# Two layers of adaptive scaling, experts and attention: border loads, table and final sums moved

## What is computed

```python
x = x + experts0(scaled_linear(x, cond))     # 8 experts, the best 2 of each token, plus shared ones
y = up(relu(down(x))) + x                    # adapter; its two weights are formed per sequence from cond
h = layernorm(y); z = y + attention(h) @ w_o + b_o
h = layernorm(z)
topv, topi = top_k(h @ gate_w + gate_b, 2); gw = softmax(topv)
x = x + z + sum over the two chosen e of gw * (relu(h @ W1[e] + b1[e]) @ W2[e] + b2[e])
```

## Time and profile before

| | |
|---|---|
| median of 3 runs | 739.51 us (737.39 to 741.89) |
| the profiled execution | 738.1 us, its span 736.3 us |
| busy share of the span | TensorE 80%, VectorE 67%, POOL 61%, ACT 50% |
| mean granted TensorE clock | 0.903 |
| moved by DMA | 115.24 MB, 157 GB/s over the span |

### The profile page before, as it was taken

One profiled execution on the slowest core, in us unless ns is written; L12 is line 12 of the kernel. 1 busy time (PEld: TensorE's weight loads), 2 busy tenths in 40 slices (PEclk: granted clock), 3 DMA queues, 4 the chain that ended last, 5 costly groups with the idle time before them and its releaser, 6 DMA issues. The chain is left out here.

```text
span 736.3 us, 17755 instructions
## 1 busy us (share of the span) xinstructions
PE 588.9 (80%) x5538; PEld 473.9 (64%) x5538; DVE 490.2 (67%) x1502; ACT 370.1 (50%) x798; POOL 448.7 (61%) x588
## 2 busy tenths in 40 slices
PE   4999935999992787737999999999920999999940
PEld 2566625989892555415766766676620999999940
DVE  3566434767671689755878878877652678878735
ACT  3444303655561344335777777777520556556520
POOL 2677741766677658274455887797763256666640
PEclk9999976999996599967999999999955899999985
DMA  7911146767773267715553444444117988888429
GB/s 223 244 57 52 55 94 163 213 198 207 201 212 103 71 187 220 222 68 104 102 119 85 132 108 132 105 125 123 44 40 162 314 258 246 260 242 248 138 66 314
DMA packets 97978, 115.24 MB, mean 157 GB/s; under 512 B 16144, under 2 KB 77616, under 8 KB 97776
## 3 DMA queue, kind: packets, MB, share of 16 engines
q1 hardware_dynamic: 82368, 92.36, 46.8%
q0 software_dynamic: 9088, 18.76, 7.8%
q10 hardware_dynamic: 6448, 3.20, 1.8%
HBM read 80.75 MB, written 33.53 MB: 155 GB/s over the span
## 5 line engine op out<-in xcount | busy, mean ns | idle before, releaser
L341 POOL DMA_INDIRECT dispatch_rows<-row,index x128 | 126.0, 984 | 56.9 <-issue 33.7
L825 POOL DMA_INDIRECT expert_rows<-fo,to x78 | 84.0, 1076 | 68.2 <-DVE fo L1883 54.8
L1570 DVE TENSOR_REDUCE mneg<-ps 128x4 f32<-128x512 f32 x128 | 86.6, 679 | 43.4 <-PE ps L1711 42.6
L825 POOL DMA_INDIRECT expert_rows<-eo,to x78 | 74.7, 958 | 52.6 <-ACT eo L918 30.2
L1661 ACT ACTIVATE prob<-ps 128x512 f32<-128x512 f32 x128 | 75.4, 589 | 54.2 <-PE ps L1723 53.5
L798 DVE CAST xh<-psT 128x256 fp32r<-128x256 f32 x78 | 33.1, 424 | 73.8 <-PE psT L766 73.6
L1872 PE MATMUL psO<-wb,fh 128*128 128x128 f32 x624 | 75.9, 275 | 0.0
L1711 PE MATMUL ps<-km,qp 96*128 96x512 f32 x128 | 63.2, 500 | 14.0 <-POOL km L1508 12.7
L1654 ACT ACTIVATE km<-kp,const 96x512 fp32r<-96x512 f32 x96 | 67.7, 712 | 11.0 <-PEq L1045 5.5
L816 PE MATMUL psA<-xh,wh 128*128 128x256 f32 (+1 forms) x234 | 73.1, 312 | 0.0
L1872 PEld LDWEIGHTS psO<-wb,fh 128*128 128x128 f32 x624 | 73.1, 192 | 0.0
(11 more groups left out here) (193 smaller groups left out, 1505.2 us busy)
## 6 DMA issues: line engine op xcount, KB each, us to landing
wb<-in_W1b SPq DMA_DIRECT2D x39, 578.0 KB
w<-in_W SPq DMA_DIRECT2D x39, 304.0 KB
qk_parts<-qk SPq DMA_DIRECT2D x8, 1024.0 KB, 5.0
qp<-qk_parts SPq DMA_DIRECT2D x48, 128.0 KB, 2.8
kp<-qk_parts SPq DMA_DIRECT2D x48, 128.0 KB, 3.4
qm<-qk_parts SPq DMA_DIRECT2D x192, 32.0 KB
xs<-dispatch_rows SPq DMA_DIRECT2D x39, 130.0 KB
xt<-dispatch_rows SPq DMA_DIRECT2D x39, 130.0 KB
```

The costliest lines, as they stand in the source:

```text
L341: pool.indirect_dma_start(out=m.xbuf, out_offset=bass.IndirectOffsetOnAxis(ap=r.index[b][:, c:c + 1], axis=0), in_=r.row[b][:, c // TOPK, ...
L825: pool.indirect_dma_start(out=m.ybuf, out_offset=bass.IndirectOffsetOnAxis(ap=to[b][:, a:a + 1], axis=0), in_=out[b][:, a, :], in_offset=N ...
L1570: nc.vector.tensor_reduce(mneg[s % 2][:, g, :], ps1[:, g % 2, :].rearrange("p (j k) -> p j k", j=4), AX_X, ALU.max, negate=True).then_inc( ...
```

## The change

It does five things.

1. **Table.** `table_vector` is cut into parts. In `layer0` the counts stand between the third gate of group 6 and the first of group 7, the experts behind that, the rows before the last gate, and the rest behind it. A new part (`table_sends`) works out how many sends of each result buffer belong to real tiles of experts 0 to 6 and of all experts. SP issues all 8 fills; ACT issues none.
2. **Border loads.** At the end of `layer0` and of `attention` SP loads the weights of tiles 0 and 1 as soon as the table is there, then waits for fills and scatters, and loads the rows of tiles 0 and 1 (`lead_loads`). The expert stages skip these. Their buffers, and those that pass from `experts0` to `pre_attention`, lie where both stages can use them (`shared_memory`, a buffer shared with attention's `prob`).
3. **Adapters.** In `experts0`, behind its tiles, SP loads the operands of groups 0 and 1, waits for the sends of the real tiles (`sends_done`), and loads these groups' rows. VectorE forms the two groups' weights and adds their rows. POOL and VectorE no longer do so in `pre_attention`.
4. **Halves.** In layer 1 a row's target is `SEQS * p + s`, plus 4096 for the expert with the higher number. So one half of `m.ybuf` is complete when the tiles of experts 0 to 6 have been sent.
5. **End.** `finish` is gone. In `experts1`, SP waits for each half's sends and loads it (4 transfers of 512 KB, pieces of 4 KB) into `m.V` and `m.X3`. VectorE adds both in place, 16 operations of 512 columns; ACT stores 8 groups of 256 KB. Some semaphores of the start are merged.

```diff
 def choose_hot(r, dve, n):
+    if r.halves:
+        nc.vector.tensor_tensor(r.later[b][:], r.choice[b][:, :, 0], r.choice[b][:, :, 1], ALU.is_gt)
...
 def index_place(r, dve, n, rank):
-    nc.vector.tensor_copy(r.row[side][:, :, :, SLOT_ID:SLOT_ID + 1].bitcast(U32),
-                          m.ids[:, n * GT:(n + 1) * GT, :].unsqueeze(3))
+    if r.halves:
+        rows = m.const[:, C_ROW:C_ROW + SEQS * TOPK].rearrange("p (s k) -> p s k", k=TOPK)
+        for k, half in ((0, float(TOK)), (1, -float(TOK))):
+            nc.vector.scalar_tensor_tensor(out=r.row[side][:, :, k, SLOT_ID].bitcast(U32), in0=r.later[b][:], scalar=half,
+                                           in1=rows[:, n * GT:(n + 1) * GT, k], op0=ALU.mult, op1=ALU.add)
...
-    table_fill(w, sp, range(E // 2))
-    sp.wait_ge(w.tails, 16 * (E + 1))
+    table_fill(w, sp, range(E))
...
+def table_sends(w, dve):
+    c(v.memset(w.real[:], 0.0))
+    for a in range(2):
+        ins = v.tensor_tensor(w.real[:, a, 0:ETILES], tl, bc(w.incl[:, E - 2 + a:E - 1 + a], P, ETILES), ALU.is_lt)
+    c(ins)
+    c(v.tensor_reduce(w.sends[:], w.real[:].rearrange("p a (i q) -> p a q i", q=OB), AX_X, ALU.add))
+    c(v.tensor_scalar(m.table[:, DONE:DONE + 2 * OB], w.sends[:].rearrange("p a q -> p (a q)"), 32.0, None, ALU.mult))
...
 # layer0, vector
+                    if n == GROUPS - 1:
+                        table_rows(tiles, dve)
                     gate(n, 2)
+                    if n == GROUPS - 1:
+                        table_sends(tiles, dve)
+                        table_end(tiles, dve)
                     if n + 3 < GROUPS:
                         scale(n + 3)
+                    if n == GROUPS - 2:
+                        table_counts(tiles, dve)
                     if n + 1 < GROUPS:
                         gate(n + 1, 0)
+                    if n == GROUPS - 2:
+                        table_experts(tiles, dve)
...
                 add(GROUPS - 1)
-                table_vector(tiles, dve)
...
+def lead_loads(m, sp, tiles, scattered, weights, w, xs):
+    sp.wait_ge(tiles.tabled, 1)
+    rows = []
+    for b in range(LEAD):
+        e = sp.value_load(m.table[0:1, b:b + 1], min_val=0, max_val=E - 1)
+        sp.dma_start(w[b], weights[bass.ds(e, 1)].rearrange("e p h -> (e p) h")).then_inc(m.ld[b], 16)
+        rows.append(sp.value_load(m.table[0:1, b + ETILES:b + ETILES + 1], min_val=0,
+                                  max_val=E * REGION + (E - 1) * SLOTS))
+    sp.wait_ge(tiles.tails, 16 * (E + 1))
+    for sem, total in scattered:
+        sp.wait_ge(sem, total)
+    for b in range(LEAD):
+        sp.dma_start(xs[b], m.xbuf[bass.ds(rows[b], SLOTS), :].rearrange("(a p) c -> p a c", p=P)).then_inc(m.ld[b], 16)
+
+def sends_done(m, sp, sent, layer, a):
+    for b in range(OB):
+        at = DONE + OB * a + b
+        sends = sp.value_load(m.table[0:1, at:at + 1], min_val=32 * (8 if a else 4), max_val=32 * 10)
+        sp.wait_ge(sent[b], sends + 32 * uses(b, OB) if layer else sends)
...
 # experts0, sync, behind the tiles
+                for b in range(2):
+                    sp.dma_start(gbu[b][:], m.gb_dram[b * GT:(b + 1) * GT, 2 * DOWN:].unsqueeze(0).to_broadcast(
+                        [DOWN, GT, 2 * P])).then_inc(m.gbu_in[b], 16)
+                sends_done(m, sp, st, 0, 1)
+                for b in range(2):
+                    sp.dma_start(rows[b][:], m.ybuf[b * GW * TOPK:(b + 1) * GW * TOPK, :].rearrange(
+                        "(t p k) c -> p t k c", p=P, k=TOPK)).then_inc(m.rows_in[b], 16)
...
 # experts0, vector, behind the tiles (four memsets of parts of wu and eight operations for both groups)
+                for b in range(2):
+                    dve.wait_ge(m.rows_in[b], 16)
+                    nc.vector.tensor_tensor(part[b][:], rows[b][:, :, 0, :], m.X[:, b * GT:(b + 1) * GT, :], ALU.add
+                                            ).then_inc(blend1, 1)
+                for b in range(2):
+                    dve.wait_ge(blend1, b + 1)
+                    nc.vector.tensor_tensor(m.x1[b], rows[b][:, :, 1, :], part[b][:], ALU.add).then_inc(blended, 1)
...
 # attention, sync, behind table_sync
+                sp.wait_ge(mixed, SEQS)
+                lead_loads(m, sp, tiles, [(sem, post.router.sends * GROUPS // 2) for sem in post.router.scattered],
+                           d["W1b"], m.late_w, m.late_xs)
...
 # experts1, sync, behind the tiles
+                for a, to in enumerate((m.V, m.X3)):
+                    sends_done(m, sp, st, 1, a)
+                    mine = m.ybuf[a * TOK:(a + 1) * TOK, :].rearrange("(p s) c -> p s c", s=SEQS)
+                    for h in range(HALVES):
+                        part = slice(h * HS1, (h + 1) * HS1)
+                        sp.dma_start(to[:, part, :], mine[:, part, :]).then_inc(upper[h] if a else lower, 16)
...
 # experts1, vector, behind the tiles
+                def blend(n, a):
+                    h, mine, rows, sem = n * GT // HS1, slice(n * GT, (n + 1) * GT), (m.V, m.X3)[a], m.blends[a]
+                    dve.wait_ge(upper[h] if a else lower, (0 if a and h else came_before) + (16 if a else 16 * HALVES))
+                    if a:
+                        dve.wait_ge(m.blends[0], GROUPS + n + 1)
+                    nc.vector.tensor_tensor(m.X[:, mine, :], rows[:, mine, :], m.X[:, mine, :], ALU.add).then_inc(sem, 1)
+                blend(0, 0)
+                for n in range(GROUPS):
+                    if n + 1 < GROUPS:
+                        blend(n + 1, 0)
+                    blend(n, 1)
...
 # experts1, scalar, behind the tiles
+                for n in range(GROUPS):
+                    act.wait_ge(m.blends[1], GROUPS + n + 1)
+                    act.dma_start(out_rows[n * GT:(n + 1) * GT].rearrange("s p c -> p s c"), m.X[:, n * GT:(n + 1) * GT, :]
+                                  ).then_inc(m.stored, 16)
```

More of the change, by code:

```diff
@@ L495, in _ @@
                 table_sync(tiles, sp)
+                lead_loads(m, sp, tiles,
+                           [(r.scattered[b], r.sends * len(range(b, GROUPS, ROW_BUFFERS))) for b in range(ROW_BUFFERS)],
+                           d["W123"], [w[:] for w in m.lead_w], [x[:] for x in m.lead_xs])
             @block.gpsimd
@@ L843, in experts0 @@
         psO = m.ps("psO0", [P, 2, 512], ctx)
-        m.ld = ld = [m.sem(f"e_ld{b}") for b in range(EB)]
+        ld = m.ld
         m.st = st = [m.sem(f"e_st{b}") for b in range(OB)]
@@ L1007, with adapter_sems @@
 PRE_LINKS = 3
+def adapter_sems(m):
+    m.rows_in = m.sems(*(f"rows_in{b}" for b in range(1 + HALVES)))
+    m.gbu_in = m.sems("p_gbu0", "p_gbu1")
+    m.mods = m.sems("p_mod1", "p_modded")
+    m.blends = m.sems("p_blend1", "p_blended")
 def pre_attention(m, d):
```

216 lines of the change are left out of this document (120 added, 96 removed).

## The result

The changed kernel takes 714.04 us (median of 4 runs, 712.37 to 715.25), the kernel before took 740.7 beside it: a ratio of 0.9637, 95% interval 0.9583 to 0.9691. Predicted were 708.3 and a range of 702 to 717. The gain is 26.7 us by the medians where 31.2 were worked out.

The account below looks back on a forecast made before the run. TensorE sets the pace inside stages, something else at the borders and end. Savings of 8.9 + 5.9 + 3.5 + 12.9 = 31.2 us from the profiled 738.1 give 706.9; the median's 1.4 more makes 708.3, range 702 to 717.

Parts of the forecast that it names:

- the four borders: The three borders between stages and the end, where TensorE has holes: 8.9 + 5.9 + 3.5 + 12.9 us saved.
- rival (a): SP's single queue bounds borders 1 and 3, fills landing 3 us later than taken in both: 714; chance 0.14.
- the four good ends: The most favourable savings at the three borders and the end: 10, 7.3, 4.5 and 14 us.
- Border 1: Dispatch to first expert stage: earlier table and weights leave only row loads behind the scatters; 8.9 us saved, 6 to 10.
- Border 2: First expert stage to adapters: early row loads, then VectorE's four additions, open the stage; 5.9 us saved, 2.2 to 7.3.
- The version kept in the range: Border 2: six padding sends each slowed 0.41 us beside VectorE's work, POOL ending 2.5 us later, leaving 4.8 of 5.9.
- Border 3: Attention to second expert stage: SP's eight fills land last, then only row loads and copies; 3.5 us saved, 2.5 to 4.5.
- The end: After the last tile: lower halves load early, then 16 additions at 0.70 us; 12.9 us saved, 9 to 14.
- (b): Early loads and padding sends delay each other; border 2 gives 2.2, the end 10: + 6.6, 715; chance 0.10.
- (c): Early waits complete only with the last tile's sends; border 2 gives 1, the end about 8: + 10, 718; chance 0.04.
- In between: Stretches between borders: two more small VectorE operations per group in attention, priced 0, at most 2.4 us; other parts 0.
- Rival (d): Layer 1 rows 16 KB apart make sends land later and VectorE wait; losing the gain takes 31 us; chance 0.03.

Follow-up runs that it names:

- the last kernel: Changed kernel plus fills on both queues, lower loads singly, POOL behind normalising, early clears, and unread TensorE products at layer ends and before tile 0: 710.24 us.

## Why the prediction was right, and where it was not

The mechanism of the four borders held; the stretches between them did not keep their length. Part of the nearness is luck. From trace to trace the gain is 23.1 against 31.2, a miss of 8.1, while the medians miss by 5.7: the prediction put the median 1.4 above the profiled execution, and for the changed kernel it lies 1.0 below. That 714 is also what rival (a) gave is chance as well, since the time went elsewhere. And the range's lower end is 1.7 us below what the four good ends give (703.7), so it was wider there than its own reason.

**Border 1 (8.9 predicted, 8.29 found, 8.95 when undone).** Right step by step, within 1.2 us. On its own axis the rows' loads left 4.1 us behind the last scatter (2.9 predicted), and from there to the first product took 4.3 us (4.9 predicted). The fills took 10.2 us instead of 8.2 and still ended before the scatters. Rival (a) is out here.

**Border 2 (5.9 predicted, 4.62 found, 5.2 when undone).** The side of VectorE was even quicker than worked out: on the axis of before its additions end at 232.5 (233.8 predicted). The step that failed is the one I had set aside for the range: that the padding's sends take their 0.96 beside VectorE's work. They took 1.60 and 2.71; 2.4 us more in sum, and POOL, not VectorE, opened the stage. The runs show it: 0.96 in all sends with VectorE's work taken away, 2.2 us gained at the border with the sends taken away, and VectorE's chain as long with them as without (8.19 and 8.26). The version kept in the range, six times the 0.41 of the earlier trace rows, gave 4.8, near the 4.62, but for another course: one of the six lost 1.75, another 0.64, the rest 0.1 or less. The Trainium skill, page "SBUF — State Buffer", section "SBUF: two separate sides", says that VectorE's two-port operations keep GpSimd from writing descriptors. The trace does not bear that out as the reason: everything that VectorE runs beside the two stretched sends is `tensor_tensor`, to which the same section gives no two-port mode, and while its clears and first products run (216.23 to 220.34) the sends took 0.95 to 1.04. Nor does an unbroken row of `tensor_tensor` always stretch a send: two of 0.96 stand beside the sixteen additions at the end. That VectorE's work did it is shown; by which operations and when is open.

**Border 3 (3.5 predicted, 2.25 found).** The fills' issue was right (8.48 us, 8.6 predicted). The mis-sized term is the way from the last scatter to the first transpose: 8.6 us where 7.4 were worked out. The last scatter was down 6.0 us after its issue, not 2.8, and the last fill 6.2 after its own, not 5.0; so SP waited for the scatter in the end, not for the fills. The rows' loads left 1.9 us later than worked out, but in two other traces they left as predicted (3.9 and 4.3) and the transpose came no sooner. The prediction took a free way for all these transfers; the weights' 1.2 MB go out right behind the fills and share the engines. Rival (a) named the place, but on the quick chip not the cause: with two queues the border was the same (10.58 against 10.63 to 10.86). On the slow kind it was 2.0 shorter, and there rival (a) was true. That on the quick chip it is the bytes fits all traces, but was not tested.

**The end (12.9 predicted, 14.16 found, 14.2 when undone).** The additions were sized at 0.70 and took 0.61 each, 1.4 us in sixteen; the halves never kept VectorE waiting. Rivals (b), for the end, and (c) are out.

**In between (0 predicted, 7.1 lost).** This is the larger miss. The sum took it that a stage in which TensorE sets the pace, or which the change does not touch, keeps its length. 2.9 us of it are the adapters: VectorE's busy time in the eight groups is 51.82 us where it was 49.12,

```profile
234.00:292.00 58.00, 45.55 (x243) 30.37 (x242) 51.82 (x136) 23.44 (x41) 34.72 (x38) 0.90 0.54 165
```

```profile
246.50:301.60 55.10, 45.61 (x243) 30.25 (x242) 49.12 (x135) 23.44 (x41) 36.72 (x38) 0.89 0.63 178
```

with the same operations: they meet POOL's at a worse moment. The normalising takes 2.2 to 3.2 us in four of the eight groups, in two before. It was seen in every kernel that has the change (56.6 to 59.3 us for eight groups, 55.1 in the one trace of before), also in the one with the adapters' part undone (58.7), so it is not that part's own price; a new phase between the engines is the reading that is left. That holding POOL back does not cure it was shown; what sets the phase was not.

1.6 us are the second expert stage: undoing the halves and the end gave 2.0 back, spreading the loads nothing. Kernels that leave this stage alone took 147.0 to 147.5 us on the first chip, where undoing gave 145.05, and 146.0 and 147.9 on the second, where the loads were spread. Rival (d), rows 16 KB apart, is not seen at its price of 31 us: in both traces of the quicker kind a pair of tiles takes 6.9 us from the third pair to the last but one. But waits for sends of 1.37 us at 586.79, where no half is being loaded, speak for a small share of it. That was not separated from the rest of the end's edit.

The 1.07 of the first expert stage and the 0.86 before attention are of the size by which the same code varies (105.3 and 106.1 us; 47.0 and 43.6). The 0.68 of attention comes back in all five traces of the quicker kind (212.4 to 212.6 us from the first reciprocal to the last scatter, 211.75 before); the prediction had named two more VectorE operations per group there and priced them at 0, at most 2.4. Undoing them on the slower kind gave nothing (222.6 against 222.7), so its cause is open.

## What to carry over

Work that is moved into another engine's idle time is only free if neither slows the other there: give each operation of POOL, descriptors too, that now falls beside VectorE's work a range, here 1 to 2.8 times its time, and ask whose end opens the next stage. Before you give a border a second queue or an earlier issue, look at how busy the transfers' engines are there: at border 3, at 0.97, both moved nothing on the quick chip, while on the slow kind the second queue brought 2.0 us. And a change that shifts stages by a few tenths of a microsecond changes which operations meet in the stages behind, so a sum over borders alone can promise too much: here by 7 us of 31, though each border was right to 1.3.

## What I had not expected of the hardware

- A send's descriptors took POOL 0.96 us alone and up to 2.71 beside VectorE's four additions (221.94 to 224.42), while these kept their 0.6 us each; beside the additions at the end a send took 0.96 again. VectorE's normalising (1.12 for four) took 2.22 beside POOL's arithmetic, and an operation of POOL's 1.71 where it otherwise takes 1.25: with tensor operations on both sides, both can lose.
- The same program took 740 us on some chips and 812 to 815 on others, the kernel before with a granted clock of 0.887 to 0.900 there and 0.899 to 0.912 on a quicker one. The products took the same 0.28 us; TensorE stood and waited in the expert stages, every second tile of the second stage's last quarter taking 5.7 and its neighbour 2.7 us where both took 3.4. The relative gain of the change was the same within the intervals.
- In the last kernel the unread products end at 105.66. TensorE's granted clock is 1.00 from 106 to 108, with no product running, 0.82 from 108 to 109 and 0.50 from 109 to 111, where the product ahead of tile 0 runs. So here the products at the layer's end did not carry the high level to the next stage, and the one ahead of tile 0 began at the low one.
